# Which queue stores a finished sequence: moving two row stores from SyncE to ScalarE, three turns earlier

## The reference, cut to what matters

```python
x = L0_attn_x                                     # (16, 256, 256) f32
x = _layernorm(x + attention(x, w_q, w_k, w_v, w_o))
# gates = softmax(x @ gating_w); the top 2 of 8 experts, each with a capacity of 1280 rows
# out[t] += weight * (relu(x[t] @ w1[e] + b1[e]) @ w2[e] + b2[e])
x = _layernorm(x + experts(x, gating_w, w1, b1, w2, b2))
```

## Time and profile before

| what | value |
|---|---|
| median of 3 runs | 905.94 us (902.3 to 907.24) |
| the profiled execution | 900.38 us |
| its span, first to last instruction | 898.6 us |
| TensorE matmul busy | 792.6 us, 88% of the span |
| VectorE busy | 569.9 us, 63% |
| ScalarE busy | 458.7 us, 51% |
| GpSimd busy | 401.1 us, 45% |

### The profile page before, as it was taken

One profiled execution on the slowest core, in us unless ns is written; L12 is line 12 of the kernel. 1 busy time (PEld: TensorE's weight loads), 2 busy tenths in 40 slices (PEclk: granted clock), 3 DMA queues, 4 the chain that ended last, 5 costly groups with the idle time before them and its releaser, 6 DMA issues.

```text
span 898.6 us, 19252 instructions
## 1 busy us (share of the span) xinstructions
PE 792.6 (88%) x7197; PEld 718.5 (80%) x7197; DVE 569.9 (63%) x1259; ACT 458.7 (51%) x889; POOL 401.1 (45%) x573
## 2 busy tenths in 40 slices
PE   5779999999999876089999999999999999999950
PEld 4656777777777654089999999999999999999950
DVE  4566888888888875444554566555545666555425
ACT  3156677776777755234443444444434444444317
POOL 1000265554565553534444445544444455444235
PEclk9789999999999998579999999999999999999985
DMA  6545656555656418152252352432523535322148
GB/s 164 89 87 107 116 130 141 109 110 131 138 120 126 98 30 280 28 199 36 42 136 47 50 139 48 112 67 42 136 46 52 138 47 118 65 39 45 20 75 334
DMA packets 70217, 90.77 MB, mean 101 GB/s; under 512 B 11980, under 2 KB 55148, under 8 KB 69996
## 3 DMA queue, kind: packets, MB, share of 16 engines
q1 hardware_dynamic: 52108, 67.69, 29.1%
q0 software_dynamic: 17408, 21.05, 14.8%
q10 hardware_dynamic: 608, 0.79, 0.4%
HBM read 37.87 MB, written 25.84 MB: 71 GB/s over the span
## 4 chain that ended last, share of the span: by engine, by line
PE 53%; ACT 2%; DMA 2%; POOL 1%; issue 1%; DVE 1%; ACTq 0%; POOLq 0%; SPq 0%; DVEq 0%
PE wide L1316 9%; PE wide L1318 9%; PE wide L1317 9%; PE bank L1339 8%; PE bank L1338 8%; PE bank L1337 8%; PE bank L1299 2%; ACT acc_sb L1227 2%; POOL acc_rows L1156 1%; POOL slot_list L481 0%; DMA acc_rows<-o_w,stack 0%; DMA acc_sb<-acc_rows 0%; DMA slot_list<-item,dest 0%; PE bank L871 0%; DMA stack<-x_rows,stack 0%
## 5 line engine op out<-in xcount | busy, mean ns | idle before, releaser
L1156 POOL DMA_INDIRECT acc_rows<-o_w,stack x80 | 140.5, 1757 | 240.4 <-ACT o_w L1219 228.0
L1316 PE MATMUL wide<-g_hi,stack 128*128 128x256 f32 x640 | 185.4, 290 | 1.4 <-DVE g_lo L1247 1.4
L1318 PE MATMUL wide<-g_hi,stack 128*128 128x256 f32 x640 | 182.0, 284 | 0.0
L1317 PE MATMUL wide<-g_lo,stack 128*128 128x256 f32 x640 | 182.0, 284 | 0.0
L1337 PE MATMUL bank<-stack,h_hi 128*128 128x256 f32 x640 | 181.1, 283 | 0.0
L1338 PE MATMUL bank<-stack,h_hi 128*128 128x256 f32 x640 | 181.1, 283 | 0.0
L1339 PE MATMUL bank<-stack,h_lo 128*128 128x256 f32 x640 | 181.1, 283 | 0.0
L780 DVE TENSOR_REDUCE negm<-wide 128x4 f32<-128x1024 f32 x128 | 155.8, 1221 | 30.5 <-PE wide L911 28.8
L574 ACT ACTIVATE probs<-wide 128x1024 f32<-128x1024 f32 x128 | 131.1, 1025 | 76.6 <-PE wide L929 72.8
L1206 ACT ACTIVATE h<-wide,b1T 128x256 f32<-128x256 f32 x320 | 133.3, 471 | 70.3 <-DVE h_hi L1257 34.5
L1219 ACT ACTIVATE o_w<-o_b,stack 128x256 f32<-128x256 f32 x80 | 36.5, 502 | 200.1 <-DVE o_b L1276 196.3
(11 more groups left out here) (170 smaller groups left out, 1385.9 us busy)
## 6 DMA issues: line engine op xcount, KB each, us to landing
stack<-qk SPq DMA_DIRECT2D x186, 128.0 KB, 3.9
w_raw<-in_L_ffn_w SPq DMA_DIRECT2D x16, 1024.0 KB, 6.2
x_sb<-in_L_attn_x SPq DMA_DIRECT2D x16, 256.0 KB, 4.3
x_rows<-x SPq DMA_DIRECT2D x16, 256.0 KB, 4.1
acc_rows<-x SPq DMA_DIRECT2D x16, 256.0 KB, 4.8
acc_sb<-acc_rows SPq DMA_DIRECT2D x8, 512.0 KB, 6.5
out<-acc_sb SPq DMA_DIRECT2D x8, 512.0 KB, 2.7
x_rows<-zrow SPq DMA_DIRECT2D x1, 1280.0 KB, 10.9
```

The lines of the kernel that those rows point to most:

```text
L1156: nc.gpsimd.indirect_dma_start(out=acc_d, out_offset=bass.IndirectOffsetOnAxis(ap=lists[:, e, QC * c + r, 0:1], axis=0), in_=o_w[c][:, r, ...
L1316: nc.tensor.matmul(out, w1_hi[:, k, f], G_hi[:, k, :], start=(k == 0), stop=False)
L1317: nc.tensor.matmul(out, w1_hi[:, k, f], G_lo[:, k, :], start=False, stop=False)
L1318: ins = nc.tensor.matmul(out, w1_lo[:, k, f], G_hi[:, k, :], start=False, stop=(k == DK - 1))
```

## The change

The two stores of x1 are taken out of SyncE's program and put into ScalarE's, behind the write of x1 in the loop body. Their offset becomes 45 for every sequence: three turns earlier for the first fifteen, and the same for the last. That is the fifth turn of the next sequences' cycle, two turns ahead of the turn of the stack copies (offset 7, remainder 7). ScalarE waits for its own write of x1 first.

```diff
-        X1, STORE, POS, SLOT = (42, 42, 43, 44), (48, 48, 48, 45), (46, 44, 45, 43), (47, 45, 45, 44)
+        X1, STORE, POS, SLOT = (42, 42, 43, 44), (45, 45, 45, 45), (46, 44, 45, 43), (47, 45, 45, 44)
@@ sync_program
-                n = routed(turn, STORE)
-                if n is not None:
-                    sp.wait_ge(x1_done, n + 1)
-                    sp.dma_start(x1_v[n], x1[n % 2][:, :, :]).then_inc(x1_stored[n % 2], 16)
-                    sp.dma_start(acc_v[n], x1[n % 2][:, :, :]).then_inc(x1_stored[n % 2], 16)
@@ scalar_program
                     ins.then_inc(x1_done, 1)
+                m = routed(turn, STORE)
+                if m is not None:
+                    act.wait_ge(x1_done, m + 1)
+                    nc.scalar.dma_start(x1_v[m], x1[m % 2][:, :, :]).then_inc(x1_stored[m % 2], 16)
+                    nc.scalar.dma_start(acc_v[m], x1[m % 2][:, :, :]).then_inc(x1_stored[m % 2], 16)
```

## The result

The changed kernel takes 938.42 us (median of 4 runs, 934.15 to 939.93), the kernel before beside it 904.12: a ratio of 1.0371, 95% interval 1.0318 to 1.0424. Ratios in this text leave out runs over 1.5% above the fastest of their kernel, which are two of the six of `hi_first` and none of any other kernel. The profiled execution's span is 932.4 us, 33.8 more than before. It is all in the first stage: the first expert's first transposes (line 1299) start at 384.35 us before and at 419.05 us after, and what follows takes as long as it did, to within 1 us. Line 929 now waits for the shift rows of each of the last twelve sequences, from 121 us on.

The account below looks back on a forecast made before the run. TensorE (18.23 us) and VectorE (16.98) were the tight pair in the 19.3 us period. Zero for SyncE, ScalarE's issue, copies and shift rows, plus 0.7 and 0.2, made +0.9 on the 905.94 median: 906.8 us, range 901.5 to 914.

Parts of the forecast that it names:

- SyncE's part: SyncE's queue behind the stack copies: losing two issues of 0.59 and 0.50 us gains nothing, as no listed consumer waits.
- ScalarE's issue: Fifth turn, before the next exponential: two store issues taken as 1.42 us, costing 0 because line 929 comes later anyway.
- Two issues go in here: ScalarE's 0.78 us idle gap after the gate exponentials end at 200.28, where the prediction placed both store issues.
- only just: Last shift row's landing before line 929: 2.7 to 3.1 us against a limit of 3.11, so cost 0.
- The shift rows' landing: Last shift-row issue to line 929: 2.7 to 3.1 us, cost 0; upper bound 3.66, costing 0.55 us for each sequence.
- Late shift rows: Slower rival at line 929, seventh turn: 0.55 us for each of twelve sequences, +7.5 to +8.2 us, up to 914; chance 0.21.
- The sum's 0 for the twelve sequences: Shift rows' term in the forecast sum: no cost at line 929 in any of twelve sequences.
- The upper end: Shift rows' landing of 3.66 us, seen with a 1 MB load behind them, costing 0.55 us for each sequence.
- The copies: Twelve stack copies sharing the DMA engines with the stores: cost nothing, with some 5 us of cover; at most 1.4 us.
- the stage's end: First stage's last sequences: stores ahead of already late shift rows cost 0 to 1.4 us, taken as 0.7.
- Slow issue: Slower rival on ScalarE: two issues take 2.18 us, 0.38 us for each of twelve sequences, +5.5, 911.4 us; chance 0.09.
- the unnamed wait: Faster rival: half of VectorE's 1.0 us waits in a period came from SyncE's queue, 6 us, 900.8 us; chance 0.06.

Follow-up runs that it names:

- hi_first: Kernel before with only the shift rows' high parts issued ahead of the wait for the low parts; ratio 1.0121.
- act_45_later: Changed kernel, but ScalarE also waits for its gate exponentials before issuing x1's stores; ratio 1.0017.
- load_again: Kernel before plus two 256 KB loads of x to unused SBUF tiles for each sequence, issued by ScalarE at offset 45, repeated on another chip; ratio 1.047.
- store_again: Kernel before plus two 256 KB stores of x1 to unused DRAM tensors for each sequence, issued by ScalarE at offset 45, repeated on another chip; ratio 1.0259.
- before_again: Kernel before, unchanged, run and profiled again on a chip where its median is 902.27 us; ratio 1.0012.
- sp_45_ahead: Kernel before with x1's stores at offset 45 on SyncE's queue, ahead of the shift rows; ratio 1.0223.
- act_48: Changed kernel with the stores back at the old offsets (48, last sequence 45) but still on ScalarE's queue; ratio 1.0009.

## Why the prediction was wrong

The prediction was 906.8 us with a range up to 914; 938.42 lies far outside.

- **SyncE's part: right.** Nothing was gained where SyncE lost two issues.
- **ScalarE's issue: right in outcome, wrong in size and place.** I took 1.42 us; it is 0.86 in the period shown and 1.05 by the medians, and the next exponential doesn't show it. The step that failed is its place: "Two issues go in here", behind the gate exponentials at 200.28. The rows at 192.33 and 192.82 show what happens instead: the store, which stands behind the gate exponentials in ScalarE's program and whose own wait for x1 was met long before, is issued 0.49 us before they begin. So the stores came 0.64 us ahead of the last shift row (0.95 in most periods) where I had them 0.28 us behind. act_45_later puts them behind it, and the loss goes, with 1.0017. That isn't yet the prediction's "only just": the stores are 0.38 to 1.3 us behind there and not 0.28, and the chip leaves 0.6 us more of slack.
- **The shift rows' landing: the rival of the right name, with the wrong upper bound.** Late shift rows had a chance of 0.21 and a price of 0.55 us for each sequence. I took that from the earlier trace rows, where the traffic is behind the shift rows in the same queue. Traffic ahead of them isn't bounded by it: landings of 3.6 to 6.4 us, waits of 2.3 us on average. The other omission is the clock, put at nothing: the price of a wait was the wait. The first cost 6.2 us in place of 3.2, with TensorE at half clock behind it, and some 10 of the 31 us lie in periods like it. The sum's 0 for the twelve sequences thus stands against 31 us.
- **The rule of the Trainium skill** ("DMA: Bandwidth & Descriptors", "Queues, rings and completion order") pointed the right way: completions wait for earlier writes of the same engine, across queues. The upper end to which I had tied it, 3.66 us, was itself too low. load_again and store_again fit it as far as any write counts, those to SBUF as well; they don't show that it is the mechanism.
- **The copies, and the stage's end:** no wait for a stack copy appears after, as predicted. At the end, line 929 waited 4.1 us for the last sequence's shift rows instead of 1.4; I had reckoned 0.7 more. The kernel before itself had 3.4 there in another profile (before_again).
- **Slow issue** and **the unnamed wait** didn't happen.

What stays open: what in a transfer holds up a small one behind it, and whether it takes GpSimd's list writes as well; what stores 0.28 us behind the last shift row would have done; and why the chips of the slower kind run the stage at 19.9 to 20.0 us a period.

## What to carry to other kernels

When a transfer is moved to a compute engine's queue, place it in time by its own waits, not by the instruction above it: ScalarE's queue ran half a microsecond ahead of the engine here, and if the order matters, it takes a semaphore. Before moving bulk traffic, list the small transfers that something waits for within a few microseconds, and keep the bulk behind them, by more than the length of an issue; a free slot on the issuing engine says nothing about that. And price a stall of TensorE by its own length and that of the slow clock behind it.

## What the runs showed of the hardware that I had not expected

- The last of four 8 KB transfers, landed after 2.3 us at most with nothing near, took 3.6 to 6.4 us with 512 KB issued 0.6 to 2.2 us before it from the other queue (at 102.32, 1.9), and 4.4 us with the same 3.05 us before it from its own. A store of 256 KB whose issue started 0.14 to 0.16 us after it went with 4.8 and 5.3 us.
- Loads from DRAM hold it up more than stores to DRAM (ratios 1.047 and 1.0259 on one chip), and copies of the same size within SBUF less than either (1.003 beside 1.0232 and 1.0108, on another).
- ScalarE's queue issued a 256 KB store in 0.37 us while an exponential was running. SyncE's took 0.59 for the same behind the stack copies, 0.43 elsewhere and 0.37 in sp_45_ahead.
- On chips where the kernel before takes 914 to 916 us, the kernels whose shift rows land in time have periods of 19.9 to 20.0 us, in act_48 at a granted clock of 1.00 (143 to 243 us). VectorE waits there for scores that TensorE seems to have finished a microsecond before. act_48:

```profile
184.53 0.50 PE L911 MATMUL wide<-stack 48*128 48x256 f32 x4 [0.44 <-issue]
186.27 1.23 DVE L780 TENSOR_REDUCE negm<-wide 128x4 f32<-128x1024 f32 x1 [1.20 <-PE wide L911]
```

The kernel before was only timed there, not profiled, so this is known of its variants alone.
